# A transformer layer on Trainium2: the next block's x split into f16 halves on VectorE and transposed by DMA in place of TensorE

## The reference

```python
x = L0_attn_hidden_states                                  # (16, 512, 512) f32
x = x + _layernorm(attn(_layernorm(x)))
x = x + _layernorm(ffn(_layernorm(x)))
# attn: q = h @ Wq_down.T @ Wq_up.T;  c = h @ Wkv_down.T;  k, v = c @ k_up, c @ v_up
#       softmax(q k / sqrt(32) - slope * distance, causal) v, then @ Wo.T
# ffn:  w = fp4 codes * group scales;  silu(h @ Wg.T) * (h @ Wu.T) @ Wd.T, then / rms
```

## Time and profile before

| | us |
|---|---|
| median of 3 runs | 2394.97 |
| lowest, highest | 2394.91, 2397.46 |
| profiled execution | 2397.13 |
| its span, first to last instruction | 2395.4 |
| mean granted clock of TensorE in it | 0.987 |

### The profile page before, as it was taken

The page is one execution under the profiler, slowest core; times in us unless marked ns, Lnnn a source line. Parts: engine busy times, 40 slices in busy tenths (PEclk is TensorE's granted clock), DMA queues, the critical chain, the costliest instruction groups (busy, mean ns, idle before and its releaser), DMA issues.

```text
span 2395.4 us, 38031 instructions
## 1 busy us (share of the span) xinstructions
PE 2332.0 (97%) x12830; PEld 1068.2 (45%) x12830; DVE 1587.0 (66%) x4407; ACT 1373.2 (57%) x3803; POOL 684.0 (29%) x948
## 2 busy tenths in 40 slices
PE   7699999999999999999999999999999999999988
PEld 3344444444444444444444444444444444444433
DVE  7867576666757667675775757666675765767543
ACT  4747466474755647466564746647475564746610
POOL 6522323122231313323132232312323131332312
PEclk9799999999999999999999999999999999999989
DMA  6020121201112130121202012120111203012000
GB/s 152 19 58 15 53 53 37 71 19 53 37 50 58 34 73 20 38 52 45 62 20 71 19 54 54 37 71 19 49 42 45 62 28 76 23 36 54 24 13 18
DMA packets 99233, 108.79 MB, mean 45 GB/s; under 512 B 22607, under 2 KB 72911, under 8 KB 99023
## 3 DMA queue, kind: packets, MB, share of 16 engines
q1 hardware_dynamic: 98174, 105.58, 16.8%
q10 hardware_dynamic: 864, 0.79, 0.2%
HBM read 38.42 MB, written 16.78 MB: 23 GB/s over the span
## 4 chain that ended last, share of the span: by engine, by line
PE 88%; DVE 4%; POOL 3%; ACT 2%; issue 2%; SPq 1%; DMA 0%; POOLq 0%; DVEq 0%
PE dense L401 65%; PE psO L606 6%; PE psO L401 4%; PE score L592 4%; PE low L575 3%; PE score L575 3%; DVE st_ln L844 1%; PE low L592 1%; ACT arena L790 1%; POOL rs_ln L1215 1%; PE low L407 1%; PE low L496 1%; PE score L496 1%; PE score L407 1%; POOL arena L1391 0%
## 5 line engine op out<-in xcount | busy, mean ns | idle before, releaser
L401 PE MATMUL dense<-arena,wgu 128*128 128x512 f16 x3872 | 923.4, 379 | 0.9 <-DVE arena L944 0.9
L401 PEld LDWEIGHTS dense<-arena,wgu 128*128 128x128 f16 x3872 | 375.0, 97 | 400.2 <-issue 10.6
L401 PE MATMUL dense<-wdn,arena 128*128 128x512 f16 x2048 | 517.4, 379 | 2.6 <-POOL arena L1328 2.6
L1328 POOL TENSOR_TENSOR arena<-late,arena 128x512 f16<-128x512 f32 x176 | 203.7, 1157 | 846.2 <-DVE arena L980 633.5
L1155 DVE CUSTOM_DVE_ANT_0 low<-low,mmax 128x128 f32<-128x128 f32 (+3 forms) x672 | 278.5, 435 | 211.2 <-PE low L575 209.9
L716 ACT ACTIVATE low<-low,ncol 128x128 f32<-128x128 f32 (+3 forms) x672 | 300.5, 447 | 118.2 <-DVE ncol L1155 109.7
L790 ACT ACTIVATE arena<-score 128x512 f32<-128x512 f32 (+3 forms) x672 | 280.0, 438 | 142.5 <-PE score L592 142.4
L716 ACT ACTIVATE score<-score,ncol 128x384 f32<-128x384 f32 x352 | 214.3, 609 | 142.4 <-DVE ncol L1155 142.2
L401 PEld LDWEIGHTS dense<-wdn,arena 128*128 128x128 f16 x2048 | 192.5, 98 | 180.9 <-issue 9.3
L1155 DVE CUSTOM_DVE_ANT_0 score<-score,mmax 128x384 f32<-128x384 f32 x352 | 213.8, 649 | 76.0 <-PE score L575 74.2
L1391 POOL TENSOR_SCALAR_AFFINE_SELECT arena<-arena 128x512 f32<-128x512 f32 x240 | 166.0, 692 | 248.9 <-ACT arena L790 247.6
(11 more groups left out here) (209 smaller groups left out, 2914.1 us busy)
## 6 DMA issues: line engine op xcount, KB each, us to landing
qst<-arena SPq DMA_DIRECT2D x384, 64.0 KB, 2.0
kst<-arena SPq DMA_DIRECT2D x186, 128.0 KB, 2.6
xin<-x SPq DMA_DIRECT2D x16, 1024.0 KB, 5.2
late<-x SPq DMA_DIRECT2D x64, 256.0 KB, 2.8
out<-late SPq DMA_DIRECT2D x64, 256.0 KB, 2.1
qst<-mrow SPq DMA_DIRECT2D x96, 8.0 KB, 1.9
wgu<-wo_t SPq DMA_DIRECT2D x1, 1024.0 KB, 13.1
wgu<-wq_down SPq DMA_DIRECT2D x1, 768.0 KB, 4.5
```

What stands on the lines that cost most here:

```text
L401: ins = nc.tensor.matmul(dst, w, a, start=first and k == 0, stop=last and k == len(tt) - 1)
L1328: nc.gpsimd.tensor_tensor(ht[:, 1, m, :], tb[:, m % 2, :], ht[:, 0, m, :], ALU.subtract).then_inc(sem["hl"], 1)
```

## The change

In steps 1 to 15 PE's transposes of x, ACT's four copies and DVE's four subtractions at the start of the step are gone (step 0 keeps them). Instead DVE, in slots 48 to 51 of the step before, writes for each tile of x the scaled high and low half in f16, in token order, behind its normalising. Tile i goes to the memory of tile i-1 of `xin`, tile 0 to a new buffer `early`, which also holds `ones`, `sizes` and `pos_part` of step 0. SP issues four transposing DMAs, one for each tile, 128x1024 f16, from there into `xt`: after `values` number 15 of 16 has been done (`xt` shares memory with `prob`) and after that tile's halves. In the steps that store outputs they stand ahead of the fourth store. PE waits for all four before job C. `ACT_UNITS` becomes the even units and all from slot 41 on, and `ROW_SLOT` goes from 4 to 10.

```diff
-ROW_SLOT, DNORM = 4, 22
-ACT_UNITS = [u for u in range(UNITS) if UNIT_SLOT[u] < AHEAD // 2 or UNIT_SLOT[u] > 40 and u % 2]
+X_BEFORE = 3
+ROW_SLOT, DNORM = 10, 22
+ACT_UNITS = [u for u in range(UNITS) if u % 2 == 0 or UNIT_SLOT[u] > 40]
...
+        early = sb("early", [P, D], f32)
+        ones = early[:, 0:P]
...
+        def x_halves(i):
+
+            return (xin[:, i - 1, :] if i else early[:, :]).bitcast(f16).rearrange("p (s d) -> p s d", s=2)
...
                 j = jobs(t)
-                if att:
-
-                    pe.wait_ge(sem["ln1"], val("ln1", t, 0) if not (isinstance(t, int) and t == 0) else 4)
+                if isinstance(t, int) and t == 0:
+
+                    pe.wait_ge(sem["ln1"], 4)
                     for c in range(KC):
                         transposes(c, lambda i: xin[:, i, P * c:P * c + P])
...
                 if att:
-                    pe.wait_ge(sem["sparefree"], val("sparefree", t, 4))
+                    if not ffn:
+                        pe.wait_ge(sem["sparefree"], val("sparefree", t, 4))
+                    else:
+                        pe.wait_ge(sem["xt"], val("xt", t - 1, 64))
...
-                if att:
+                if not ffn:
                     for c in range(KC):
                         high_spare(c, xt[:, 0, c, :], S_X)
...
-                if att:
+                if not ffn:
                     for c in range(KC):
                         low("P1", c, xt[:, 1, c, :], S_X, xt[:, 0, c, :])
...
                         dve.wait_ge(sem["rs"], val("rs", t, norm_of_x(ffn)))
-                        normalise("ln1", xin[:, i, :], xin[:, i, :], i).then_inc(sem["ln1"], 1)
+                        link(t, normalise("ln1", xin[:, i, :], xin[:, i, :], i))
+                        linked(t)
+                        if i:
+                            dve.wait_ge(sem["ln1"], val("ln1", t, i))
+                        elif ffn:
+                            dve.wait_ge(sem["xt"], val("xt", t - 1, 64))
+                        else:
+                            dve.wait_ge(s_row, 1)
+                        link(t, nc.vector.tensor_scalar(x_halves(i)[:, 0, :], xin[:, i, :], S_X, None, ALU.mult))
+                        linked(t)
+                        nc.vector.scalar_tensor_tensor(x_halves(i)[:, 1, :], xin[:, i, :], S_X, x_halves(i)[:, 0, :],
+                                                       ALU.mult, ALU.subtract).then_inc(sem["ln1"], 1)
...
+                def x_transposed():
+                    sp.wait_ge(sem["pv"], val("pv", t, NG * NT - 1))
                     for i in range(NT):
-
+                        sp.wait_ge(sem["ln1"], val("ln1", t, i + 1))
+                        sp.dma_start(xt.rearrange("p s c l -> p (s c) l")[:, :, P * i:P * i + P],
+                                     x_halves(i).rearrange("p s d -> p (s d)"), transpose=True).then_inc(sem["xt"], 16)
+                if not ffn:
+                    x_transposed()
+                if ffn:
+                    for i in range(NT):
+                        if nxt and i == X_BEFORE:
+                            x_transposed()
                         sp.wait_ge(sem["po"], val("po", t, i + 1))
                         sp.dma_start(out[t - 1, P * i:P * i + P, :], stage[:, i % 2, :]).then_inc(sem[f"out{i % 2}"], 16)
```

More of the change, by code:

```diff
@@ L40 @@
 COUNTS = {
-    "dense": (0, 13, 43, 43), "freev": (0, 9, 35, 35), "freea": (0, 4, 8, 8), "spare": (0, 4, 8, 8),
-    "sparefree": (0, 4, 8, 8), "hi": (0, 13, 17, 17),
+    "dense": (0, 13, 43, 43), "freev": (0, 9, 35, 35), "freea": (0, 4, 8, 8), "spare": (0, 4, 4, 4),
+    "sparefree": (0, 4, 4, 4), "hi": (0, 13, 13, 13), "xt": (0, 64, 64, 0),
     "mx": (0, 64, 64, 64), "low": (0, 64, 64, 64), "rowsum": (0, 64, 64, 64), "ln": (0, 2, 2, 2), "mh": (0, 2, 2, 2),
@@ L49 @@
     "po": (0, 0, 4, 4), "out0": (16, 0, 32, 32), "out1": (16, 0, 32, 32), "tanh": (0, 0, 11, 11), "hh": (0, 0, 11, 11),
-    "hl": (0, 0, 11, 11), "chain": (8, 23, 60, 52), "guess": (0, 2, 2, 2), "series": (0, 14, 14, 14),
+    "hl": (0, 0, 11, 11), "chain": (8, 31, 68, 52), "guess": (0, 2, 2, 2), "series": (0, 14, 14, 14),
 }
@@ L220, in layer_program @@
         steep_scale = sb("steep_scale", [P, 1], f32)
-        sizes = sb("sizes", [P, 2 * MI, GROUPS], f32)
-        pos_part = sb("pos_part", [P, 2 * MI, GROUPS], f32)
+        early = sb("early", [P, D], f32)
+        ones = early[:, 0:P]
+        sizes = early[:, P:P + 2 * MI * GROUPS].rearrange("p (a b) -> p a b", b=GROUPS)
+        pos_part = early[:, P + 2 * MI * GROUPS:P + 4 * MI * GROUPS].rearrange("p (a b) -> p a b", b=GROUPS)
         rows_of = sb("rows_of", [P, 4, 2 * MI], f32)
@@ L227, in layer_program @@
         h_scale = sb("h_scale", [P, MI], f32)
-        ones = sb("ones", [P, P], f32)
         down_divisor = sb("down_divisor", [P, KC], f32)
@@ L513, in ffn_up @@
                     for c in range(KC if m == 0 and not up else 0):
-                        pe.wait_ge(sem["sparefree"], val("sparefree", t, (4 if att else 0) + c + 1))
+                        pe.wait_ge(sem["sparefree"], val("sparefree", t, c + 1))
                         ins = products(bank(t, n)[:, :], tt[3 * c:3 * c + 3], c == 0, c == KC - 1)
@@ L929, in step @@
                 n_spare = [0]
-                his = {"P1": 0, "C": 4, "Q": 5, "K": 7, "Q1": 11, "X2": 13 if att else 0}
+                his = {"P1": 0, "C": 4, "Q": 5, "K": 7, "Q1": 11}
+                if ffn:
+                    his = {"C": 0, "Q": 1, "K": 3, "Q1": 7, "X2": 9 if att else 0}
                 def low(kind, i, dst, scale, hi):
```

## The result

The changed kernel takes 2451.09 us (median of 4 runs, 2449.21 to 2451.94) against 2394.94 for the kernel before, measured beside it. The ratio is 1.0231, with a 95% interval of 1.0214 to 1.0249: 2.3% slower, where 2365 us, 1.2% faster, was forecast.

What follows compares the result with a forecast made beforehand. PE was taken to bound steps 1 to 15. Removing transposes (-27.0 us) and step 0's new sharing (-3.0), with DMAs and DVE's work at no cost, came off the 2394.97 us median: 2365 us, range 2355 to 2440.

Steps and rivals of the forecast that it cites:

- The bound: Steps 1 to 15: PE is the path, busy 142.23 of 142.30 us in a step.
- The transposes, 1.80 us for 16: PE between values() and Wo, steps 1 to 15: removing sixteen transposes saves 1.80 us a step, 27.0 us in all.
- The DMAs fit the window of 12.3 us: SP before PE's job C: four transposing DMAs take some 7 to 11 us, within 12.3 us, costing nothing; chance 0.58.
- the second rival: PE before job C: DMAs take over 14.1 us; at 19 us, 2467 us, up to 2557 with lowered clock; chance 0.25.
- The upper end, 19 us: Transposing DMAs: upper bound from 4096 pieces at 67 ns each, 17.1 us, plus about 2 us for issue and landing.
- "Cost: nothing" for DVE's added work: DVE, slots 48 to 51: 5.3 us of added work is absorbed by later idle time, so it costs nothing.
- The cover I named: DVE's idle time of 7.62 us ending at 1127.37, said to absorb the added work with 2.3 us left.
- a sign of being wrong: DVE's idle time before the third split of oc gone, listed among what would show the prediction wrong.
- the third: Step 0 gives back its gain (+5) and DVE's work pushes a late chain: within 0.2% of before; chance 0.04.
- The size of DVE's added work, 5.3 us: DVE, slots 48 to 51: four multiplications and subtractions, 4.5 us, plus some 0.2 us per tile for waiting.
- The clock: PE behind a 6.8 us wait at job C: clock might fall to 1.2 GHz, up to 90 us more, in the second rival.
- Step 0, -3 us: Step 0: sharing weight units anew and moving the column sum takes 3 us off, between -6 and +5.

Runs made afterwards that it cites:

- the version with late splits: The changed kernel with x's normalising and splitting in slots 52 to 55 in place of 48 to 51; 2368.86 us, ratio 0.9888 to the kernel before.
- the run with one split: The kernel before, transposes kept, with DVE also splitting only x's first tile into a buffer that nothing reads; 2420.31 us, ratio 1.0102.

## Why the prediction was wrong

**The bound.** Right: in steps 1 to 15 PE was the path, and whatever it lost or gained went to the total one for one.

**The transposes, 1.80 us for 16.** Right, and shown alone by the version with late splits: 142.41 - 140.61 = 1.80 us a step. The pitch was the right measure and not the printed 273 ns.

**The DMAs fit the window of 12.3 us.** Right. DMA issues of the changed kernel from 1160 to 1175 us, with the median time to landing at the end, and SP's timeline:

```profile
DMA packets 4800, 2.10 MB, mean 140 GB/s; under 512 B 4288, under 2 KB 4288, under 8 KB 4800
...
q1 hardware_dynamic: 4800, 2.10, 56.4%
...
arena<-xin SPq DMA_TRANSPOSE x3, 3.3
arena<-early SPq DMA_TRANSPOSE x1, 3.5
...
1162.38 1.27 SPq L1524 DMA_TRANSPOSE arena<-early  x1
1163.69 4.09 SPq L1524 DMA_TRANSPOSE arena<-xin  x3
```

The last is issued at about 1166.5 and lands at 1169.8, 7.4 us behind the first issue, within the 7 to 11 us that I had taken. PE asks at about 1174.6, 12.2 us behind the first issue. The kernel did come out slower, but not for the reason that the second rival gave. The upper end, 19 us, was too high. A packet of this stretch takes 15 x 16 x 0.564 / 4800 = 28 ns on average. Among them are the 4096 packets of 256 bytes that I had supposed, and by the trace's packet records one of these takes 20 ns and not the 67 ns of a 909-byte one. The 1309 ns a block of the Trainium skill (VectorE: DVE Perf Modes, The three transpose paths) would make 41.9 us one after another, an estimate from that page; the 32 blocks took 7.4 us together. The measurement decides: the 256-byte packets, 4096 x 20 ns = 82 us of work, were all done within 5.0 us, so they ran side by side on the 16 DMA engines.

**"Cost: nothing" for DVE's added work.** This is the step that failed. I summed the work as 5.3 us and found an idle time that absorbs it (7.62 us). Then I wrote that what is queued behind it "feeds nothing that PE asks for before 1127". I had followed y's second normalising to its consumer, the output, and stopped there. Its consumer on POOL, the addition L1334, has masks queued behind it, and PE asks for the first at 1122.19. The trace before showed each link: POOL waiting 1.07 us at L1334 for L1055, the mask behind it, and 0.7 us of margin. An idle time that comes later absorbs work only for those who ask later. The cover I named ends at 1127; the demand came at 1122. Its being gone, which I had named as a sign of being wrong, didn't show either. In the changed kernel it is 6.38 us, but some 5.5 of them (3.84 + 1.7, an estimate) are there only because PE was late itself, and `oc` with it:

```profile
1010.08 0.43 DVE L1000 TENSOR_SCALAR arena<-oc 128x512 f16<-128x512 f32 x1 [6.38 <-ACT oc L722]
```

I had given nearly the right price if the cover were gone ("up to 5.3 us per step"; it was 4.0 and, in most steps, the clock's 1.7). But its only place in the rivals was the third, DVE's work pushing a late chain, with chance 0.04 and a time within 0.2% of before.

**The size of DVE's added work, 5.3 us.** Too small: the eight new instructions of the step that ends at 1019.44 took 7.35 us, as some of them are slower beside POOL (last section). The three tiles ahead of L1070 took 5.0 us in place of the 4.0 that my price gives, so about 1 us of the loss, an estimate from these rows, is this size and not the order.

**The clock.** I had tied this second loss to late DMAs alone. A wait of 3.84 us brought a fall in twelve of fourteen steps, of 3.4 us in eleven and 6.8 us in one. Waits of 0.84 and 0.68 us in one step, in the run with one split, brought none.

**Step 0, -3 us.** Wrong in size. Without its transposes step 0 should have ended at 139.89 or, with the 3 us, at 136.9; it ended at 142.49, which is +2.6 and inside the -6 to +5 that I had allowed. With late splits it ended at 139.62, so -0.3. The sharing anew does bring 4.1 us there (143.73 without it, 139.62 with it), but the rest of the change costs step 0 about as much (143.73 after 139.89), and the splits in slots 48 to 51 another 2.9 us (142.49 after 139.62). PE waits there too, once 3.1 us for a low half that DVE writes. The prediction had named this danger, DVE's splits holding up PE, for step 0 alone.

## What to carry to other kernels

When work is added to an engine off the path, an idle time behind it is no proof that it is free: list every instruction queued behind it, follow each to its consumer, and there again list what is queued behind that consumer. The smallest margin on all these ways counts, here 0.7 us by way of a third engine, and not the sum of busy time. If a change loses although its main parts cost what they should, move the added work by a few places before giving the change up: one number turned 2.3% slower into 1.1% faster.

## What the runs showed of the hardware

DVE and POOL slow each other. The new multiplication to f16 takes 0.43 us alone and 1.37 us beside POOL's addition (so in all 28 cases of the changed kernel), and the addition takes 1.27 us alone and 1.43 to 1.49 in these cases. The subtraction takes 0.69 alone and 1.00 to 1.06 beside a mask. Timeline of the changed kernel:

```profile
991.11 1.44 POOL L1360 TENSOR_TENSOR late<-late 128x512 f32<-128x512 f32 x1
...
991.45 1.37 DVE L1215 TENSOR_SCALAR early<-xin 128x512 f16<-128x512 f32 x1
...
992.50 0.82 POOL L1417 TENSOR_SCALAR_AFFINE_SELECT arena<-arena 128x512 f32<-128x512 f32 x1
992.86 1.00 DVE L1217 SCALAR_TENSOR_TENSOR early<-xin,early 128x512 f16<-128x512 f32 x1
```

The multiplication ends 0.3 us behind POOL's addition, as if it had stood still for most of it. The Trainium skill (SBUF — State Buffer, Who interferes with whom) says that DVE and GpSimd share one pair of ports, and that against a DVE instruction in a two-port mode whoever issues first has the pair for its whole instruction while the other blocks. The trace agrees in part: the later one waits, but the first, POOL's addition, is slower too, by 0.17 us. So a tile's split cost 2.4 us in its worst place, twice the 1.12 of the rows I had used. No run here separates this slowdown from the order of the queues.

A transposing DMA of 128x1024 f16 keeps SP's queue for 1.27 to 1.34 us in the step shown (up to 3.0 us elsewhere in the run), where a plain one beside it takes 0.34 to 0.43. It lands 3.4 us behind its issue at the median, 3.1 to 5.7 us over the run.
